# A first feed-forward in two parts, with the attention's opening among its slots, on one Trainium2 core

## What is computed

```python
x = x + 0.5 * ffn0(layernorm(x))        # 8 experts; each token goes to the best one
x = x + relative_attention(layernorm(x))  # 16 heads, d = 8, bucketed relative positions
x = x + 0.5 * ffn0(layernorm(x))        # the same experts again
x = x + 0.5 * spline_ffn(layernorm(x))
x = x + causal_attention(layernorm(x))
x = x + 0.5 * spline_ffn(layernorm(x))

def ffn0(t):                      # t: 2048 x 128
    p = softmax(t @ switch_w + switch_b); e = argmax(p)
    y = gelu(t @ w1[e] + b1[e]) @ w2[e] + b2[e]
    return y * max(p)

scores = (q @ k.T + c2p + p2c) / sqrt(24)   # c2p, p2c: position terms by distance bucket
out = layernorm(softmax(scores) @ v @ Wo + bo + hidden)
```

## Time and profile before

| | us |
|---|---|
| median of 3 runs | 754.83 (754.27 to 755.80) |
| the profiled execution | 755.21 |
| its span, first to last instruction | 753.0 |
| PE / DVE / ACT / POOL busy | 574.0 / 526.4 / 443.7 / 193.0 |
| mean granted PE clock | 0.889 of full |

### The profile page before, as it was taken

The page is one execution under the profiler, slowest core; times in us unless marked ns, Lnnn a source line. Parts: engine busy times, 40 slices in busy tenths (PEclk is TensorE's granted clock), DMA queues, the critical chain, the costliest instruction groups (busy, mean ns, idle before and its releaser), DMA issues. The chain is left out here.

```text
span 753.0 us, 16635 instructions
## 1 busy us (share of the span) xinstructions
PE 574.0 (76%) x5242; PEld 407.7 (54%) x5242; DVE 526.4 (70%) x1839; ACT 443.7 (59%) x952; POOL 193.0 (26%) x252
## 2 busy tenths in 40 slices
PE   4249967539999999999999998352995771678880
PEld 3249853225666666766667676242985441346550
DVE  7414237726779888998999994872225799777797
ACT  3215525327788888998899995650552534376723
POOL 1704425102901720470310000053443200211200
PEclk9999987878999999999999998655998796799785
DMA  9648634999999999999944422734553000000001
GB/s 241 174 136 276 226 99 132 291 310 335 272 383 297 231 353 335 230 216 316 309 136 132 117 61 70 194 84 140 169 170 117 0 1 0 0 1 0 1 0 56
DMA packets 124326, 124.46 MB, mean 165 GB/s; under 512 B 25162, under 2 KB 102770, under 8 KB 123346
## 3 DMA queue, kind: packets, MB, share of 16 engines
q1 hardware_dynamic: 115666, 95.72, 47.0%
q0 software_dynamic: 3872, 25.58, 8.7%
q10 hardware_dynamic: 4704, 2.11, 1.0%
HBM read 67.91 MB, written 47.80 MB: 154 GB/s over the span
## 5 line engine op out<-in xcount | busy, mean ns | idle before, releaser
L1535 DVE CUSTOM_DVE_ANT_0 l0am_prob<-l0am_ps_s,l0am_bias 128x512 f32<-128x512 f32 x256 | 166.6, 689 | 40.8 <-PE l0am_ps_s L1615 20.3
L1455 ACT ACTIVATE l0am_prob<-l0am_prob,l0am_neg_top 128x512 f32<-128x512 f32 x256 | 171.4, 723 | 14.7 <-DVE l0am_neg_top L1535 14.7
L1628 PE MATMUL l0am_ps_t<-c_ident,l0am_prob 128*128 128x128 f32 x1024 | 128.9, 275 | 0.9 <-DVE l0am_probT L1522 0.4
L1628 PEld LDWEIGHTS l0am_ps_t<-c_ident,l0am_prob 128*128 128x128 f32 x1024 | 110.8, 141 | 16.0 <-issue 7.9
L591 ACT ACTIVATE l0f_h<-l0f_psU,l0f_experts 128x128 f32<-128x128 f32 x184 | 52.4, 368 | 84.4 <-PE l0f_psU L887 70.9
L1615 PE MATMUL l0am_ps_s<-l0am_ks,l0am_qs 32*128 32x512 f32 x512 | 74.5, 647 | 14.1 <-DVE l0am_neg_top L1535 11.9
L1522 DVE COPY l0am_probT<-l0am_ps_t 128x512 f32<-128x512 f32 x128 | 82.1, 683 | 1.5 <-PE l0am_ps_t L1628 1.4
L1449 ACT COPY l0am_probT<-l0am_ps_t 128x512 f32<-128x512 f32 x128 | 68.6, 589 | 12.9 <-PE l0am_ps_t L1628 12.9
L763 DVE COPY l0f_xsT<-l0f_psT 128x128 f32<-128x128 f32 x46 | 13.4, 292 | 83.9 <-PE l0f_psT L877 66.6
L1642 PE MATMUL l0am_ps_cg<-l0am_probT,l0am_v 128*9 128x128 f32 x2048 | 67.9, 273 | 2.5 <-DVE l0a_heads L1546 2.5
L502 POOL DMA_INDIRECT token_results<-l0f_ys,l0f_token_i x46 | 44.2, 962 | 81.9 <-DVE l0f_ys L773 79.6
(11 more groups left out here) (322 smaller groups left out, 959.4 us busy)
## 6 DMA issues: line engine op xcount, KB each, us to landing
l0am_bias<-near_terms SPq DMA_DIRECT2D x128, 192.0 KB, 6.1
near_terms<-l0am_near POOLq DMA_DIRECT2D x6, 3072.0 KB, 13.8
l0f_mine<-l0f_experts SPq DMA_DIRECT2D x46, 256.0 KB
near_terms<-l0am_near SPq DMA_DIRECT2D x2, 3072.0 KB, 11.4
l0am_rows_k<-position_k SPq DMA_DIRECT2D x12, 512.0 KB, 8.4
l0f_experts<-in_L_ffn_w SPq DMA_DIRECT2D x2, 2048.0 KB, 9.4
l0f_experts<-in_L_ffn_w SPq DMA_DIRECT2D x16, 256.0 KB, 4.8
position_q<-l0am_rows SPq DMA_DIRECT2D x16, 256.0 KB, 5.8
```

Of the source, the lines that this page charges most:

```text
L1455: nc.scalar.activation(prob[:, k, :], prob[:, k, :], ACT.Exp, bias=neg_top[:, k:k + 1], scale=-1.0)\
L1535: dve.tensor_tensor_reduce(out=prob[:, k, :], in0=ps_s[:, j, :], in1=bias[:, j, at:at + S], scale=-1.0, scalar=HUGE, op0=ALU.add, op1=ALU.min,
L1628: last = pe.transpose(ps_t[:, BANK_OF[j], i, :], prob[:, u % SLOTS_, i * P:(i + 1) * P], ident[:, :])
```

## The change

The first feed-forward runs in two parts: tiles 0 to 3 (batch 0) and tiles 4 to 15. Each part has its own regions in `sorted_tokens` and its own slots, 4 + 7 = 11 and 12 + 7 = 19, so there are 30 slots where 23 were. Part 0 is counted and laid out between the sets of the opening; part 1 is counted in DVE's iteration 0 and laid out in iteration 1 of the slot loop. ACT writes the eight blank tiles of part 0 as before, POOL scatters those of part 1 behind the results of slots 0 to 7. The second feed-forward keeps one part.

`extend` is cut in its two sides and the bias, placed in PE's slots 12, 13 and 14. A new object, `AttentionOpening`, does batch 0's opening: POOL loads batch 0's results after slot 11, DVE adds them to x and takes statistics in slot 17 and normalises in slot 19, ACT takes the root in slot 18 (another activation table), PE transposes in slot 20 and multiplies one chunk in each of the iterations 21 to 30, ACT copies a chunk in slots 21 to 29 and one behind them, SP stores them from its iteration 24 on, and POOL and SP load the rows for `near` back, by groups of four heads (POOL groups 0 and 1, SP groups 2 and 3).

In the attention block DVE now builds `near` first and adds the results of batches 1 to 3, normalises and takes the values behind it. `near` is stored in four pieces of four heads. ACT, PE and SP keep batch 1's ten chunks there.

The diff, cut to its core:

```diff
+FIRST_PART = 4
+PARTS_OF = {1: ((0, TILES, 0),), 2: ((0, FIRST_PART, 1), (FIRST_PART, TILES, 2))}
...
+        EXTEND_SLOT, GATHER_SLOT, UPDATE_SLOT = 12, STARTS[1], STARTS[1] + 6
+        TURN_SLOT = UPDATE_SLOT + 3
+        PRODUCT_SLOTS = range(TURN_SLOT + 1, TURN_SLOT + 1 + BATCH_CHUNKS)
+        STORE_SLOTS = range(PRODUCT_SLOTS[0] + 3, ALL_SLOTS)
+        LOAD_SLOTS = range(PRODUCT_SLOTS[0], PRODUCT_SLOTS[0] + 2 * TABLE_CHUNKS)
...
-                for s in range(SLOTS):
+                for s in range(ALL_SLOTS):
...
+                    if opening and s in STORE_SLOTS:
+                        cn = STORE_SLOTS.index(s)
+                        opening.store_chunk(sp, cn)
+                        if cn >= 2:
+                            opening.load_rows(sp, cn - 2, (2, 3), opening.other_rows_in)
...
+                    if opening and s < EXPERTS:
...
+                        pool.indirect_dma_start(
+                            xs_dram[:, :], bass.IndirectOffsetOnAxis(ap=blank_i[:, 1, s:s + 1], axis=0),
+                            c["blank"][:, s, 0:XS_COLS], None).then_inc(later_blanked[s], 16)
+                    if opening and s == GATHER_SLOT:
+                        for j in range(UNROLL):
+                            pool.wait_ge(ys_out[j], 16 * len(range(j, STARTS[1], UNROLL)))
+                        opening.gather(pool, ys_dram, 0)
+                    if opening and s in LOAD_SLOTS:
+                        opening.load_rows(pool, LOAD_SLOTS.index(s), (0, 1), opening.first_rows_in)
...
+                    if opening and s == UPDATE_SLOT + 1:
+                        opening.deviate(act)
...
+                    if opening and s in PRODUCT_SLOTS:
+                        opening.copy_rows(act, PRODUCT_SLOTS.index(s))
...
+                    count_slots(0)
                     choose(1)
...
+                    place_slots(0)
                     choose(2)
...
+                    if opening and s == 0:
+                        count_slots(1)
+                    if opening and s == 1:
+                        place_slots(1)
+                        dve.wait_ge(rows_ready, 2)
+                    if opening and s == UPDATE_SLOT:
+                        opening.update(dve)
...
+                    if opening and s in (EXTEND_SLOT, EXTEND_SLOT + 1):
+                        aside.extend(pe, s - EXTEND_SLOT)
+                    if opening and s == EXTEND_SLOT + 2:
+                        aside.multiply_bias(pe)
...
-                if aside:
-                    aside.extend(pe)
...
-                for cn in range(2 * TABLE_CHUNKS):
-                    store_chunk(cn)
-                    if cn >= 2:
-                        load_half_rows(sp, 0, cn - 2)
...
+                for b in range(1, B):
+                    opening.gather(sp, ys_dram, b)
...
                 sp.wait_ge(near_dve, 1)
                 store_first_near(0)
-                load_rows(1, 0)
-                load_rows(1, 1)
+                for cn in range(BATCH_CHUNKS, BATCH_CHUNKS + ROW_BUFS):
+                    store_chunk(cn)
                 sp.wait_ge(filled, 1)
                 sp.wait_ge(first_near_out[0], 16)
                 for t in range(T4):
                     load_bias(0, t)
...
+                        if n == 1 and t % 2 == 0:
+                            store_first_near(2 + t // 2)
...
-                statistics(0, T4)
-                normalise(1, 0, T4)
...
                 near_build(dve, 0, between).then_inc(near_dve, 1)
+                done(opening.add_results(dve, 1))
+                statistics(T4, 2 * T4)
+                normalise(1, T4, 2 * T4)
+                opening.add_results(dve, 2)
+                done(opening.add_results(dve, 3))
+                statistics(2 * T4, TILES)
+                normalise(2, 2 * T4, TILES)
```

More of the change, by code:

```diff
@@ L795, in _ @@
                     late.shape(dve)
-                for b in range(B):
+                for b in range(0 if opening else B):
                     dve.wait_ge(gathered[b], 16)
@@ L1398, in _ @@
                     if b == 1:
-                        for half in range(2):
-                            pool.wait_ge(first_near_out[half], 16)
+                        for g in range(GROUPS):
+                            pool.wait_ge(first_near_out[g], 16)
                     near_build(pool, b, between).then_inc(near_pool, 1)
```

457 lines of the change are left out of this document (284 added, 173 removed).

## The result

| | before | changed |
|---|---|---|
| median | 754.55 (4 executions) | 773.07 (770.60 to 777.66) |
| ratio, first comparison | 1 | 1.0268 (1.0197 to 1.0339) |
| ratio, second comparison | 1 | 1.0248 (1.0192 to 1.0304) |
| span of the profiled execution | 753.0 | 768.9 |
| PE / DVE / ACT / POOL busy | 574.0 / 526.4 / 443.7 / 193.0 | 590.3 / 531.5 / 454.0 / 213.1 |

The change is slower by 2.5 to 2.7%, some 19 us, where 7.4 us (1%) and at most 769 were forecast. The profiled execution of the changed kernel, 770.6, is the lowest of its four, so the traces differ by 15.9 us only. A few single executions that stood far above the others of their kernel are left out of them.

What follows compares the result with a forecast made beforehand. PE was taken to hold the slot loop, with PE and DVE waiting through most of the chain to the first quad. Terms 29.3 - 7.3 - 12.8 - 2.8 + 1 = +7.4 us gave 762.0, range 750 to 769.

Steps and rivals of the forecast that it cites:

- End of the feed-forward: Last result to attention block: load and adds go, landing, block change and POOL's queue stay, 4.7 for 11.97 us: -7.3.
- Quad 16: In the quads: POOL's building for batch 1 waits for piece 3 of `near` and starts later: +1 us (0 to 6).
- The rival on batch 1's `near`: In the quads: piece 3 is held up on one queue, quad 16 waits 5 us more: 767; chance 0.11.
- The extension: Iterations 12 to 14: 4.99 us of PE work plus two PE stops of 1.9 us waiting for ACT's copies: +8.8.
- The start: Start of the slots: they open earlier as part 0 is laid out between the sets: -3 us (gain 0 to 5.5).
- The stretch to the last result: First turn to last result: slots, extension, products, root, update and gaps taken up, together +32.3 us.
- Slots and products: Slot loop: seven more slots at 2.10 us, +14.7; transposes and ten chunk products in iterations 20 to 30, +9.4.
- the first rival: Slot loop: extension and products lie in time a slot has anyway, making the kernel faster: 751.1; chance 0.31.
- To the first quad: Attention block's start to first quad: `near` 13.4 us, then 26.5 to the first addition, 39.9 for 52.68: -12.8.
- The root: ACT in slot 18: two activation table loads of 1.28 us plus 0.3, about 1 on PE's path: +0.9 (0 to 2.9).
- the rival that the change doesn't do what it says: Slot 17 on: batch 0's results late, loop stops, row loads unlanded, `near` late: 4 to 6 us, 767; chance 0.08.
- POOL's clearing: Attention block: POOL clearing `near` and `bias` blocks DVE building `near`, up to some 6 us: 768; chance 0.06.

Runs made afterwards that it cites:

- the cover run: Changed kernel with the results of batches 1 to 3 loaded and added at the feed-forward's end again, not in the attention block; ratio 1.0217.
- the second trace of before: The kernel before, profiled once more with nothing changed; ratio to itself 1.0016.
- e15: Changed kernel with the extension in slots 12, 14, 16, results of batches 1 to 3 added at the feed-forward's end, `near` pieces one behind the other; ratio 1.0058.
- the three edits: Changed kernel with rows loaded by SP alone, extension in slots 12, 14, 16, results of batches 1 to 3 added at the feed-forward's end; ratio 1.0137.

## Why the prediction was wrong

- **End of the feed-forward: the step that failed most.** The prediction kept "the landing of the last results, 2.93, the change of block, 0.83, and about 0.9" for POOL's queue. It read the end of before from DVE's rows alone. POOL's drain of 3.24 us was under them and in no row chosen; uncovered, and 5.86 long, it stands where the loads and adds stood. Measured +0.6 for -7.3. Of the 7.9 us between them 5.9 are the drain, a term that the sum did not have, and 1.9 are POOL's queue and landing, 5.77 us where the prediction had 2.93 and 0.9. Shown by the cover run: the loads and twelve adds fit under the drain for nothing.
- **Quad 16: right rival, wrong size.** "+1 (0 to 6)" assumed that POOL starts "about 5 us later" against the first quad; it was 12.7 later (29.8 for 17.1), since piece 3 left SP's queue only at 201.35, nine other transfers behind piece 2 (190.23). The rival on batch 1's `near` priced it rightly (5 us) and had 0.11; it came on top of the forecast's other miss. The run with the pieces one behind the other shows the cause: POOL starts 17.3 us behind the first quad, and quad 16 waits 0.85.
- **The extension.** Stops 2.03 and 1.94 for 1.9 each. The slower clock behind them, 4.9 us in this trace and 3.7 in the second, had no term: +8.8 should have been 12.5 to 13.7.
- **The start** was under-rated: about 6 us like with like, for 3, and outside the 0 to 5.5 given; a start before 42 was among the prediction's own signs of being wrong. It took ACT's eight blanks at 12.15 us from the late trace; in the changed kernel they took 8.47 (from 28.02), as in the second trace of before (from 30.45). The start hid the clock's cost: the last result, at 127.4, was even earlier than the forecast 131.4, which is luck.
- **The stretch to the last result** came out at +35.0 for +32.3, and at +32.1 between the two second traces (89.6 for 57.5 us). As the clock's cost is in it and had no term, other terms were some 2 to 4 us too large; no run tells which.
- **Slots and products** held: 2.0 to 2.3 us a slot for 2.10, and slots with a product 2.75 us apart for 2.8. So the first rival (the loop hides the work), with 0.31, is out. But of the seven slots' 14 to 16 us only about 9 (5 to 13) reached the kernel's time when they stood alone: waits further on gave up the rest.
- **To the first quad** held: 26.6 us behind `near` for 26.5, released by PE as said.
- **The root** cost what the row said. ACT's timeline in the changed kernel:

```profile
91.78 1.28 ACT L1249 ACT_TABLE_LOAD   x1
93.08 0.30 ACT L1249 ACTIVATE l0o_newton<-l0o_mv,c_eps 128x4 f32<-128x4 f32 x1
93.94 1.28 ACT L642 ACT_TABLE_LOAD   x1 [0.56 <-PE l0f_psU L968]
```

- **The update** held: DVE took batch 0's results at 89.62 without a wait for them, and PE then waited 0.90 and 0.37 us for DVE, 1.3 for the 1.5 of the sum. `near` began at the block's start, so the rival that the change doesn't do what it says (0.08) is out.
- **POOL's clearing** beside DVE's `near` cost nothing: 3.03 + 10.36 as before, from 139.68 with the MEMSETs from 139.57 to 147.8. That rival (0.06) is out.
- **The base.** The sum stood on a trace whose slots began 3.6 us late. The medians of before in the comparisons are 751 to 753; the median change, 19 us, is therefore some 3 us more than the traces' 15.9.

What stays open: how much of the 20 us by which e15's last result is late could be hidden in another order, what besides the stops makes the clock fall, and how much more than the adds' end keeps the three edits from giving more than one (1.0137 for 1.0129, intervals of 0.4 points each way).

## What to carry to other kernels

Before the work at the end of a block is moved away, list every engine's own end there, the drains too: the work that goes may have been the cover of something that stays, and that something grows with what the change adds to that engine. For a stop of a busy PE, look in a trace for a slower stretch behind it, and take its price from there. What is put under a drain is checked again when the drain becomes shorter. And a gain at the head of a chain counts only after the next transfer that was sent later for it has been followed to the quad that needs it.
